# Thirteen transfers with long rows in place of 32 that fill a head's stacks, and the key differences and their low part taken in two successive groups

## The reference

```python
x = x + attn(layernorm(x))
# attn, for each batch b and head h
q, k, v = h @ Wq.T, h @ Wk.T, h @ Wv.T        # (2048, 64) each
scores  = q @ k.T + bias[bucket(k_pos - q_pos)]
ctx     = softmax(scores) @ v                  # then @ Wo.T
```

## Time and profile before

| | us |
|---|---|
| time, median of 3 runs | 4181.5 (4177.5 to 4183.55) |
| the profiled execution: time, span | 4169.57, 4167.8 |
| busy PE, POOL, DVE, ACT | 3766.1, 2678.3, 2448.8, 1989.7 |
| mean granted clock of PE | 0.958 |

### The profile page before, as it was taken

One profiled execution on the slowest core, in us unless ns is written; L12 is line 12 of the kernel. 1 busy time (PEld: TensorE's weight loads), 2 busy tenths in 40 slices (PEclk: granted clock), 3 DMA queues, 4 the chain that ended last, 5 costly groups with the idle time before them and its releaser, 6 DMA issues. The chain is left out here.

```text
span 4167.8 us, 64834 instructions
## 1 busy us (share of the span) xinstructions
PE 3766.1 (90%) x21277; PEld 2217.3 (53%) x21277; DVE 2448.8 (59%) x3356; ACT 1989.7 (48%) x3452; POOL 2678.3 (64%) x1402
## 2 busy tenths in 40 slices
PE   8989998989999898899998889998997999997899
PEld 6844444444444444444444444444444888885477
DVE  3466656655656565556656555656652777775642
ACT  3335555555555554555555555555553455553322
POOL 1138888878888887788888878888896344441010
PEclk9989999999999999999999999999999999999999
DMA  8632223332222253322223332222232233335720
GB/s 227 164 90 61 61 62 70 85 81 62 65 61 61 65 157 87 70 64 63 61 62 71 82 84 61 66 61 61 61 106 82 79 106 99 103 99 173 250 79 21
DMA packets 407284, 367.05 MB, mean 88 GB/s; under 512 B 199579, under 2 KB 271771, under 8 KB 405784
## 3 DMA queue, kind: packets, MB, share of 16 engines
q1 hardware_dynamic: 337976, 336.54, 31.4%
q10 hardware_dynamic: 67168, 20.98, 2.2%
q0 software_dynamic: 1920, 6.29, 0.5%
HBM read 142.64 MB, written 89.70 MB: 56 GB/s over the span
## 5 line engine op out<-in xcount | busy, mean ns | idle before, releaser
L344 POOL TENSOR_TENSOR acc<-acc,probs 128x1024 f32<-128x1024 f32 x894 | 2125.4, 2377 | 517.9 <-ACT probs L802 324.6
L932 DVE TENSOR_REDUCE maxes<-ps 128x2 f32<-128x1024 f32 x1024 | 1251.9, 1223 | 784.2 <-PE ps L601 765.4
L805 ACT ACTIVATE probs<-ps,far_bias 128x1024 f32<-128x1024 f32 (+7 forms) x1280 | 997.6, 819 | 1142.2 <-DVE near_s L949 617.6
L632 PE MATMUL ps<-probs,v_head 128*64 128x512 f32 x4096 | 1045.0, 633 | 6.9 <-ACT ctx_out L788 4.9
L620 PE MATMUL ps<-stacks 64*128 64x512 f32 x6144 | 814.3, 393 | 1.8 <-ACT probs L802 1.8
L601 PE MATMUL ps<-stacks 64*128 64x512 f32 x2048 | 520.2, 506 | 303.2 <-DVE maxes L932 279.0
L601 PEld LDWEIGHTS ps<-stacks 64*128 64x128 f32 x2048 | 196.8, 189 | 888.1 <-DVE maxes L932 672.3
L620 PEld LDWEIGHTS ps<-stacks 64*128 64x128 f32 x6144 | 587.4, 188 | 127.6 <-ACT probs L802 7.5
L632 PEld LDWEIGHTS ps<-probs,v_head 128*64 128x64 f32 x4096 | 257.3, 141 | 475.2 <-issue 470.8
L949 DVE TENSOR_TENSOR near_s<-ps,near_bias 128x384 f32<-128x384 f32 (+2 forms) x576 | 262.2, 489 | 37.7 <-PE ps L620 37.3
L802 ACT ACTIVATE probs<-near_s 128x384 f32<-128x384 f32 (+2 forms) x576 | 273.6, 475 | 0.0
(11 more groups left out here) (278 smaller groups left out, 4502.7 us busy)
## 6 DMA issues: line engine op xcount, KB each, us to landing
stacks<-c_k SPq DMA_DIRECT2D x512, 128.0 KB, 2.4
stacks<-c_q SPq DMA_DIRECT2D x256, 128.0 KB, 2.4
stacks<-c_d SPq DMA_DIRECT2D x256, 128.0 KB, 2.4
scr_v<-probs ACTq DMA_DIRECT2D x32, 512.0 KB, 4.1
v_head<-scr_v SPq DMA_DIRECT2D x32, 512.0 KB, 3.6
scr_ctx<-ctx_out SPq DMA_DIRECT2D x128, 128.0 KB, 2.3
both_ctx<-scr_ctx SPq DMA_DIRECT2D x32, 512.0 KB, 3.9
sums<-scr_inv SPq DMA_DIRECT2D x126, 128.0 KB, 2.9
```

The lines of the kernel that those rows point to most:

```text
L344: pool.tensor_tensor(acc[:, qb, :], acc[:, qb, :], pr, ALU.add).then_inc(s["summed"], 1)
L632: mm = pe.matmul(ps[64 * half:64 * half + 64, PV, :], v_head[:, side, kt, :], probs[:, st % PT_RING, half * 512:(half + 1) * 512], start=k ...
L805: ins = act.activation(probs[:, st % PT_RING, a:z], sc[:, a:z], ACT.Exp, bias=bias)
L932: dve.tensor_reduce(maxes[:, qt:qt + HALF_GROUPS // 2 + 1:HALF_GROUPS // 2, first_chunk + pair], ps[:, bank:bank + 2, :], AX.X, ALU.max).t ...
```

## The change

fill becomes 13 transfers: in a first pass over blocks 0 to 2 and a second over block 3, two of high keys (64 x 1536 or 64 x 512) and the high queries of each half with blocks in it; then two of low queries (64 x 2 x 512), two of differences and two of low parts (64 x 2048 each). take_out, keys_out and queries_low move to the projection's own group (2, 6, 10, 14), step and step_hi to the next (3, 7, 11, 15), and step_lo stays in 4, 8, 12, 0, now ahead of the second maximum. For block 3, step and step_hi come in the last group of head n, where they stood in the first of head n+1.

```diff
--- before.py
+++ after.py
@@ -66,8 +66,9 @@
 
 TERMS = [(k, i, j) for k in range(KT) for i, j in ((0, 0), (0, 1), (1, 0))]
 PROJ_GROUPS = {4 * tb + 2: (tb, 0, len(TERMS)) for tb in range(BLOCKS)}
-EVAC_GROUPS = {4 * tb + 3: tb for tb in range(BLOCKS)}
-SPLIT_GROUPS = {4 * (tb + 1) % GROUPS: tb for tb in range(BLOCKS)}
+EVAC_GROUPS = {4 * tb + 2: tb for tb in range(BLOCKS)}
+STEP_GROUPS = {4 * tb + 3: tb for tb in range(BLOCKS)}
+LOW_GROUPS = {4 * (tb + 1) % GROUPS: tb for tb in range(BLOCKS)}
 FIRST_MAX, LAST_MAX = 3, 2
 SUM_GROUPS = {13: 0, 5: 1}
 RECIP_GROUPS = {14: 0, 6: 1}
@@ -104,7 +105,7 @@
 
 QUARTERS = 4
 QUARTER, QP = QW // QUARTERS, P // QUARTERS
-FILLS_MAX, FILLS_SCORE, FILLS_GUARD = 16 * 3 * BLOCKS, 16 * 5 * BLOCKS, 32
+FILLS_MAX, FILLS_SCORE, FILLS_GUARD = 16 * 7, 16 * 6, 32
 CHUNKS = S // 512
 
 
@@ -225,6 +226,18 @@
             homes[n] for n in "wo wo_hi wo_lo wq2 wk2 wv2 enc bv bk k2 v2 ctx x bq".split()]
 
 
+        def queries(stacks, side, half, at, first, count):
+
+            blocks = stacks[lane(half), side, QS, at:at + QL].rearrange("p (b n) -> p b n", n=512)
+            tb = first + (half - first) % 2
+            return blocks[:, tb // 2:tb // 2 + count, :]
+
+        def own_queries(rows, half, first, count):
+
+            blocks = rows.rearrange("p (b a n) -> p a b n", a=2, n=512)
+            tb = first + (half - first) % 2
+            return blocks[:, half, tb // 2:tb // 2 + count, :]
+
         def proj_bank(m, tb):
 
             return (PB, SC, SC + 1, MX + 1)[tb] if isinstance(m, int) and m == 0 else PB
@@ -399,22 +412,22 @@
                 past(sp, s["scored"], (m - 1) * STEPS)
                 if isinstance(m, int) and m == 1:
                     sp.wait_ge(s["vps"], N_HALVES)
-                for tb in range(BLOCKS):
-                    cols = slice(tb * 512, (tb + 1) * 512)
-                    q_high = slice(tb // 2 * 512, (tb // 2 + 1) * 512)
-                    sp.wait_ge(s["k_hi"], 4 * m + tb + 1)
-                    sp.wait_ge(s["step_lo"], 4 * m + tb + 1)
+                for first, end in ((0, BLOCKS - 1), (BLOCKS - 1, BLOCKS)):
+                    cols = slice(first * 512, end * 512)
+                    sp.wait_ge(s["k_hi"], 4 * m + end)
+                    sp.wait_ge(s["step_lo"], 4 * m + end)
                     for half in range(2):
                         sp.dma_start(stacks[lane(half), side, KH, cols].bitcast(F32), c_k[0:64, cols]).then_inc(s["fill_max"], 16)
-                    sp.dma_start(stacks[lane(tb % 2), side, QS, q_high].bitcast(F32), c_q[0:64, cols]).then_inc(s["fill_max"], 16)
-                for tb in range(BLOCKS):
-                    cols = slice(tb * 512, (tb + 1) * 512)
-                    own = slice(LOOKBACK + tb * 512, LOOKBACK + (tb + 1) * 512)
-                    q_low = slice(QL + tb // 2 * 512, QL + (tb // 2 + 1) * 512)
                     for half in range(2):
-                        sp.dma_start(stacks[lane(half), side, KD, cols].bitcast(F32), c_d[0:64, own]).then_inc(s["fill_score"], 16)
-                        sp.dma_start(stacks[lane(half), side, KL, cols].bitcast(F32), c_k[64:128, cols]).then_inc(s["fill_score"], 16)
-                    sp.dma_start(stacks[lane(tb % 2), side, QS, q_low].bitcast(F32), c_q[64:128, cols]).then_inc(s["fill_score"], 16)
+                        count = len(range(first + (half - first) % 2, end, 2))
+                        if count:
+                            sp.dma_start(queries(stacks, side, half, 0, first, count).bitcast(F32), own_queries(c_q[0:64, :], half, first, count)).then_inc(s["fill_max"], 16)
+                for half in range(2):
+                    sp.dma_start(queries(stacks, side, half, QL, 0, 2).bitcast(F32), own_queries(c_q[64:128, :], half, 0, 2)).then_inc(s["fill_score"], 16)
+                for half in range(2):
+                    sp.dma_start(stacks[lane(half), side, KD, :].bitcast(F32), c_d[0:64, LOOKBACK:]).then_inc(s["fill_score"], 16)
+                for half in range(2):
+                    sp.dma_start(stacks[lane(half), side, KL, :].bitcast(F32), c_k[64:128, :]).then_inc(s["fill_score"], 16)
 
             def divisors(n, qb):
 
@@ -842,15 +855,10 @@
                     if own:
                         exp(n, k, side, 2 * g)
                         exp(n, k, side, 2 * g + 1)
+                    if prep and g in STEP_GROUPS:
+                        step_hi(n + 2, STEP_GROUPS[g])
                     if prep and g in EVAC_GROUPS:
                         take_out(n + 2, EVAC_GROUPS[g])
-                    if g in SPLIT_GROUPS:
-                        tb = SPLIT_GROUPS[g]
-                        if tb < BLOCKS - 1 and prep:
-                            step_hi(n + 2, tb)
-                        if tb == BLOCKS - 1 and own and nxt:
-                            step_hi(n + 1, tb)
-                    if prep and g in EVAC_GROUPS:
                         keys_out(n + 2, EVAC_GROUPS[g])
                     if g == 0 and carry:
                         values_out(n - 1, 1)
@@ -1021,24 +1029,24 @@
                     first_head()
                     return
                 for g in range(GROUPS):
-                    stepped = None
-                    if g in SPLIT_GROUPS:
-                        tb = SPLIT_GROUPS[g]
+                    lowered = None
+                    if g in LOW_GROUPS:
+                        tb = LOW_GROUPS[g]
                         if tb < BLOCKS - 1 and prep:
-                            stepped = (n + 2, tb)
+                            lowered = (n + 2, tb)
                         if tb == BLOCKS - 1 and own and nxt:
-                            stepped = (n + 1, tb)
+                            lowered = (n + 1, tb)
                     if has_max(n, g):
                         largest(n, side, g, 0)
                     if own:
                         near(n, k, side, 2 * g)
                         near(n, k, side, 2 * g + 1)
-                    if stepped:
-                        step(*stepped)
+                    if prep and g in STEP_GROUPS:
+                        step(n + 2, STEP_GROUPS[g])
+                    if lowered:
+                        step_lo(*lowered)
                     if has_max(n, g):
                         largest(n, side, g, 1)
-                    if stepped:
-                        step_lo(*stepped)
                     if prep and g in EVAC_GROUPS:
                         queries_low(n + 2, EVAC_GROUPS[g])
                     if isinstance(n, int) and n == NH - 1:
```

## The result

The changed kernel takes 4269.6 us (median of 4, 4267.5 to 4272.4) against 4182.5 (4 runs): ratio 1.021, 95% interval 1.0192 to 1.0228, slower by 87 us. The forecast was 4232, slower by 50. The whole interval lies above 1, so the kernel is slower; whether by more than 2% it does not settle. The two profiled spans differ by 102.8 us (4270.6 and 4167.8): the profiled execution of before (4169.6) was faster than all four timed ones (4177.5 and up), while that of the changed kernel was the slowest of its four.

What follows compares the result with a forecast made beforehand. The fill's end and TensorE's queued work were taken to bound each head; +4.2 + 0.4 - 2.3 - 0.6 = +1.7 us per head, +51 us over 30 heads, gave 4232.5 us; own range 4195 to 4275, 8-in-10 range 4160 to 4285.

Steps and rivals of the forecast that it cites:

- The direction: Whole kernel: slower than before, given a chance of 0.66, against 0.19 for faster and 0.15 for the same.
- step 2: Group 3 of a head: block 0's copies move to group 2, so TensorE stops with less work queued, +4.2 us per head.
- step 5: VectorE's passes, one per group instead of two or three: smaller TensorE waits go, -0.6 us per head (bounds 0 and -1.8).
- Step 1: Fill of the stacks: takes 21.1 us from first issue, ending 2.3 us earlier per head (bounds 1.1 and 2.8).
- Step 3: From the end of the fill back to TensorE: guard's reduction +0.2 and step_lo in group 4 +0.2, together +0.4 us.
- Step 4: TensorE's clock after the wait: the 2.0 us loss per head stays unchanged, within half a microsecond either way.
- Step 6: Lead-in, where the first fills wait for three blocks at once: 0, within 4 us, once.
- (a): Fill: long rows run at twice the rate, 390 GB/s, -9.1 us per head, about 3909 us; chance 0.13.
- (d): Fill: ends no earlier, as a 512 KB transfer waits for its slowest engine; +4.0 us per head, 4301; chance 0.08.
- the coalescing rule: Fill: coalesce small transfers into a large one; its fit would put the fill at some 11.6 us; cited under (a).

Runs made afterwards that it cites:

- e2: The changed kernel with the old 32 fill transfers, so the new groups alone; 4287.2 us, ratio to before 1.0259.
- e1: The kernel before with the 13 merged transfers only, take_out, step and step_lo in their old groups; 4162.4 us, ratio 0.9956.
- e4: The changed kernel with its last four transfers (differences, low parts) over 128 partitions instead of 64, same bytes; 4165.4 us, ratio 0.9959.
- e9: The changed kernel with eight transfers of 256 KB instead of four of 512 KB for differences and low parts; 4252.1 us, ratio 1.0169.
- e10: The kernel before with the merged fill and blocks 1 to 3 in the changed order, block 0 at its old places; 4159.5 us, ratio 0.9952.
- e11: The kernel before with merged fill, split fill waits, block 0's step_lo in group 5, blocks 1 to 3 in changed order; 3938.1 us, ratio 0.9419.
- e12: e11 with the high parts of the first two fills issued block by block, later fills merged; 3926.5 us, ratio 0.9394.
- e3: The changed kernel with block 0's copies back in group 3, its step and step_lo both in group 4; 4180.2 us, ratio 0.9998.

## Why the prediction was right and where it was short

**The direction and step 2, work ahead of the wait: right.** e2 carries only the new groups and costs 106 us, 3.5 per head. The gap begins behind scores 7, as forecast, and 4.3 us earlier in the head shown (22.1 to 17.8). In the mean it is 4.7 (22.9 to 18.2): the 4.2 us of work and half a microsecond of short waits at the head's start that went (step 5).

**Step 1, the end of the fill: the mechanism right, the size too large.** This is the term that was mis-sized. Forecast: 2.3 us sooner. Measured: 0.95 (23.3 to 22.4), below my bound of 1.1, and only about half of it is the merge's: 0.4 in e1, 0.5 from e2 to the changed kernel. The other 0.45 came with the new groups, in e2 with the old transfers; why is open.

The limit by 64 partitions holds (e4). The section on the port swizzle, which the Trainium skill has in "SBUF — State Buffer", gives about 218 GB/s as the asymptote for 64 partitions. The window of 20 us shows 218 too, but as a mean; the rows of 8 KB alone went above it, at 233, and there the measurement decides.

The gap in the share did close: over the fill of the heads shown it rose from 0.85 to 0.96. But I counted as if all that the engines move were the stacks', and 0.5 MB more of it was not. SP was through with the stacks 6 us sooner and queued the loads of values and biases behind them, and engines that had finished their part of the stacks went on to these loads while others still moved rows of 8 KB: in the head shown the first packet of 4 KB starts 19.6 us after the first issue, the last one of 8 KB 20.9 us after it. At 219 GB/s 0.5 MB is an estimated 2.2 us of all engines, against the 1.35 that are missing. That uneven end is what I left out; halving the pieces gives 0.5 us back (e9), and the rest was not separated. The first stretch is also slower, 189 GB/s at share 0.94 while the 6 KB rows of high keys move, against 203 at 0.92 before; the cause of that is open. 1.35 us missing in 30 heads are 40 us, more than the 37 between forecast and result.

**Step 3, the way back to TensorE: nearly.** Copy to resume takes 2.70 us against 2.61, where the guard's reduction alone was to give 0.2. The other 0.2, for step_lo in group 4, would lie behind the resume and was not measured by itself.

**Step 4, the clock: right.** Eight value products take 3.68 us in both kernels, and TensorE's busy time on the two pages is 3766.1 and 3769.5 us, a tenth of a microsecond per head apart.

**Step 5, the smaller waits: wrong.** Forecast -0.6 per head; e10 and e11 show -0.1. The waits themselves did shrink: summed over the heads in the profiles, TensorE's idles of 0.1 to 3 us are 2.60 per head in e1 and 2.22 in e10. The head became no shorter by it, and the timelines show where it went. In e10 TensorE reaches its gap 0.5 us sooner than in e1 (22.9 and 22.45 us into the head), but it resumes only 0.3 sooner, since the end of the fill decides there: 0.2 went into the gap. The other 0.3 came back behind the gap, as longer idles for the most part; their cause is open.

**Step 6, the lead-in: wrong by 5 us.** The first guard product starts at 275.2 instead of 266.4. I gave it "0, within 4"; it is +9, once. The first pass, which waits for three blocks, is one cause: e12, which differs from e11 in that alone, starts 7.8 us sooner. It is not the only one: in e2, which has the old fill, the first guard product starts at 271.0, 4.6 us late, and in e1, which has only the merge, at 274.3, 7.9 late. The two parts do not add up, and the share of each in the changed kernel is open.

**The sum.** By place in the head, means over the same 28 heads in us:

| | before | changed |
|---|---|---|
| first guard product to first issue of the fill | 3.83 | 3.38 |
| fill, first issue to copy | 23.31 | 22.35 |
| copy to TensorE's resume | 2.61 | 2.70 |
| resume to the next head | 62.27 | 66.69 |
| head | 92.03 | 95.12 |

I had the first row as unchanged; it falls by 0.45, and goes with the new order of the blocks, since e2, e3 and e10 have it and e1 has not. The fourth row has the 4.2 us of step 2 and 0.2 more. In all a head is 3.1 us longer where I forecast 1.7; 30 heads are 93 us, the lead-in gives 9, and the profiled spans differ by 103. My sum started from that same profiled execution, so in its own terms it had +51 for +103, half of what came. Between the medians the loss is only 87, because the median of before lies 13 us above its profiled execution, and that of the changed kernel does not. That the result stands as near to the forecast as it does, and inside the forecast's own range of 4195 to 4275, near its upper end, is in part luck. This range is also narrower than what its bounds give when all are taken together, 4185 to 4302.

**The rivals.** (a), the double rate with long rows, fell: the rows of 8 KB moved at 233 GB/s, not 390, and all transfers together, over the fill, at 219. The 13 issues took 15.6 us, not the 8 that I had for a limit by issue alone; as I read it, SP was held while the data engines worked off what it had queued (last section). What the coalescing rule promises (the Trainium skill, "DMA: Bandwidth & Descriptors", rules for kernel authors) came to 18 us of 4180 (e1). (d) was near: the uneven end did eat more than half of the gain.

## What to carry to other kernels

When an engine waits in order, ask what the engine it feeds still has queued: issuing the waiting instruction earlier moves the stall in front of work that used to hide it, here 4.2 us per head. Before making a transfer faster, look at which of its bytes the waiting instruction really needs: a semaphore per buffer gave 184 us on top of the merge where merging gave 18. And the share of the data engines next to their GB/s tells how much fewer and longer transfers can still gain: here it was 0.92 in the full stretches, and merging gave 0.4% of the time. When SP gets through sooner, ask also what it queues next, and whether those bytes compete with the ones waited for.

## What the runs showed of the hardware

Transfers inside SBUF ran at 212 GB/s (rows of 2 KB) and 233 (rows of 8 KB) over 64 partitions and at 389 over 128 (rows of 4 KB), at a full share in all three (e4, changed kernel). Two issues of 512 KB took SP 4.48 us where two of 128 KB had taken 1.14. The size alone does not explain it: the load of values, 512 KB in every kernel, took a median of 0.43 us to issue before, 2.02 behind the fill with the largest pieces and 0.47 behind that of e9. That a queue still full holds SP is my reading of it. Larger pieces are not always better: 17 transfers beat 13 by 17.5 us.
